# One VectorE maximum over two PSUM banks in place of one per bank, second context attention of a Perceiver kernel

## The reference

```python
q = (query @ Wq).reshape(b, sq, NUM_HEADS, HEAD_DIM).transpose(0, 2, 1, 3)   # 256 rows, 32 heads of 32
k = (key @ Wk).reshape(b, sk, NUM_KV_HEADS, HEAD_DIM).transpose(0, 2, 1, 3)  # 4096 context rows, 8 heads of 32
v = (value @ Wv).reshape(b, sk, NUM_KV_HEADS, HEAD_DIM).transpose(0, 2, 1, 3)
scores = jnp.einsum('bhqd,bhkd->bhqk', q, k) * scale                         # each key head serves 4 query heads
probs = jax.nn.softmax(scores, axis=-1)
out = jnp.einsum('bhqk,bhkd->bhqd', probs, v)
```

## Time and profile before

| | |
|---|---|
| time, median of 3 runs | 2255.72 us (2251.92 to 2257.29) |
| profiled execution: its time | 2258.47 us |
| profiled execution: its span | 2257.0 us |
| granted TensorE clock, mean over the span | 0.957 |
| VectorE maxima L1794 | 512 instructions, first at 1324.0 us, last at 1923.5 us |

### The profile page before, as it was taken

The page is one execution under the profiler, slowest core; times in us unless marked ns, Lnnn a source line. Parts: engine busy times, 40 slices in busy tenths (PEclk is TensorE's granted clock), DMA queues, the critical chain, the costliest instruction groups (busy, mean ns, idle before and its releaser), DMA issues.

```text
span 2257.0 us, 27306 instructions
## 1 busy us (share of the span) xinstructions
PE 2052.8 (91%) x10908; PEld 1502.6 (67%) x10908; DVE 1370.9 (61%) x2070; ACT 843.4 (37%) x1169; POOL 244.4 (11%) x131
## 2 busy tenths in 40 slices
PE   7899999999979999999989767999999999978978
PEld 5799999999968787877778644433333333356843
DVE  3454454454447878797666466666676667266455
ACT  2111111111126666656535212444434443735421
POOL 0000000000006555544000010000000000010000
PEclk9999999999989999999999878999999999989889
DMA  5443343342257656655443161011101110026042
GB/s 178 157 123 117 100 123 117 100 123 79 82 155 212 198 189 200 216 187 178 122 156 120 47 223 38 1 28 29 28 1 28 29 22 7 19 80 245 12 159 86
DMA packets 127869, 243.43 MB, mean 108 GB/s; under 512 B 16525, under 2 KB 79361, under 8 KB 120449
## 3 DMA queue, kind: packets, MB, share of 16 engines
q1 hardware_dynamic: 127745, 241.71, 34.5%
HBM read 177.70 MB, written 63.86 MB: 107 GB/s over the span
## 4 chain that ended last, share of the span: by engine, by line
PE 80%; DVE 11%; DMA 4%; ACT 3%; issue 2%; SPq 0%; POOL 0%; DVEq 0%; ACTq 0%
PE psum L1668 10%; PE psum L467 10%; PE psum L1636 7%; PE psum L1654 4%; PE psum L448 4%; PE psum L450 4%; PE psum L449 3%; PE psum L435 3%; PE psum L277 3%; PE psum L279 3%; PE psum L278 3%; DVE top L1794 3%; PE psum L812 3%; PE psum L814 2%; PE psum L813 2%; PE psum L827 2%
## 5 line engine op out<-in xcount | busy, mean ns | idle before, releaser
L1794 DVE TENSOR_REDUCE top<-psum 128x1 f32<-128x512 f32 x512 | 338.9, 688 | 142.6 <-PE psum L1636 140.8
L1735 ACT ACTIVATE probs_f<-psum 128x1024 f32<-128x1024 f32 x256 | 255.1, 1023 | 308.4 <-PE psum L1654 308.0
L600 DVE TENSOR_REDUCE top<-psum 128x2 f32<-128x512 f32 x272 | 186.5, 691 | 198.1 <-PE psum L435 197.9
L1636 PE MATMUL psum<-k_rows,q_rows 96*128 96x512 f32 x512 | 233.6, 484 | 50.1 <-DMA k_rows<-k_low 22.2
L1668 PE MATMUL psum<-probs_f,v_all 128*64 128x512 f32 x1024 | 274.0, 629 | 0.0
L1636 PEld LDWEIGHTS psum<-k_rows,q_rows 96*128 96x128 f32 x512 | 94.9, 197 | 232.1 <-DVE top L1794 179.3
L903 DVE TENSOR_TENSOR probs_low<-probs,probs_high 128x1024 fp32r<-128x1024 f32 x136 | 194.1, 1432 | 76.8 <-ACT probs L866 76.6
L865 ACT ACTIVATE probs_high<-psum 128x1024 fp32r<-128x1024 f32 x136 | 139.9, 1028 | 161.2 <-PE psum L814 148.3
L448 PE MATMUL psum<-c_high,w_high 128*128 128x256 f32 (+1 forms) x672 | 190.7, 284 | 3.2 <-issue 3.2
L449 PE MATMUL psum<-c_low,w_high 128*128 128x256 f32 (+1 forms) x672 | 190.6, 284 | 0.0
L450 PE MATMUL psum<-c_high,w_low 128*128 128x256 f32 (+1 forms) x672 | 190.5, 284 | 0.0
(11 more groups left out here) (356 smaller groups left out, 3701.3 us busy)
## 6 DMA issues: line engine op xcount, KB each, us to landing
wf_rows<-in_ffn_w_dram SPq DMA_DIRECT2D x42, 512.0 KB, 4.2
staged<-in_ctxT_dram SPq DMA_DIRECT2D x32, 512.0 KB, 5.1
wf_rows<-in_ffn_w_dram SPq DMA_DIRECT2D x8, 1376.0 KB, 7.6
q_dram<-wf_turned SPq DMA_DIRECT2D x42, 256.0 KB, 2.3
gate_up<-q_dram SPq DMA_DIRECT2D x10, 1024.0 KB, 8.1
value_high<-v_high SPq DMA_DIRECT2D x32, 256.0 KB, 3.7
value_low<-v_low SPq DMA_DIRECT2D x32, 256.0 KB, 4.6
k_rows<-k_high SPq DMA_DIRECT2D x16, 512.0 KB, 6.9
```

What stands on the lines that cost most here:

```text
L600: dve.tensor_reduce(top0[:, r0:r0 + 2, n], psum[:, bank, :].rearrange("p (i n) -> p i n", i=2), AX_X, ALU.max).then_inc(*b.bank_read.up())
L1636: pe.matmul(psum[:, bank, :], q_rows[0:3 * HD1, kv, rows * P:(rows + 1) * P], k_rows[kv % 2][0:3 * HD1, chunk * BANK:(chunk + 1) * BANK], ...
L1735: act.activation(probs[n % 4][:], psum[:, 2 * (n % 2):2 * (n % 2) + 2, :].rearrange("p b n -> p (b n)"), ACT.Exp, scale=scale).then_inc(*f ...
L1794: dve.tensor_reduce(top1[:, rows, chunk:chunk + 1], psum[:, 6 + m % 2, :], AX_X, ALU.max).then_inc(*f.max_read.up())
```

## The change

The even job of each two no longer waits for a single bank and no longer signals. It waits until VectorE has read both banks of the pair of jobs before; the odd job follows without a wait and signals for both. VectorE does nothing at even jobs and at odd ones reduces both banks in one instruction of 128 x (2 x 512) into two columns of `top1`. Counts of the semaphores are halved. The order of the calls on PE and the number of matmuls stay as they are.

```diff
@@ tensor_program, maximum @@
-                    if made >= 2:
-                        pe.wait_ge(*f.max_read.at(made - 1))
-                    pe.matmul(psum[:, bank, :], q_rows[0:3 * HD1, kv, rows * P:(rows + 1) * P],
-                              k_rows[kv % 2][0:3 * HD1, chunk * BANK:(chunk + 1) * BANK], start=True,
-                              stop=True).then_inc(*f.max_made.up())
+                    if m % 2 == 0 and made >= 2:
+                        pe.wait_ge(*f.max_read.at(made // 2))
+                    done = pe.matmul(psum[:, bank, :], q_rows[0:3 * HD1, kv, rows * P:(rows + 1) * P],
+                                     k_rows[kv % 2][0:3 * HD1, chunk * BANK:(chunk + 1) * BANK], start=True, stop=True)
+                    if m % 2:
+                        done.then_inc(*f.max_made.up())
                     made += 1
@@ vector_program, maximum @@
                     rows, chunk = divmod(m, NC1)
+                    if m % 2 == 0:
+                        return
                     read += 1
                     dve.wait_ge(*f.max_made.at(read))
-                    dve.tensor_reduce(top1[:, rows, chunk:chunk + 1], psum[:, 6 + m % 2, :], AX_X,
+                    dve.tensor_reduce(top1[:, rows, chunk - 1:chunk + 1], psum[:, 6:8, :], AX_X,
                                       ALU.max).then_inc(*f.max_read.up())
```

## The result

| | before | after |
|---|---|---|
| time, median | 2256.51 us (2251.92 to 2258.04, 4 runs) | 2595.59 us (2591.27 to 2621.42, 4 runs) |
| ratio, 95% interval | | 1.153 [1.1453, 1.1608] |
| span of the profiled execution | 2257.0 us | 2597.0 us |
| granted TensorE clock | 0.957 | 0.876 |

The account below looks back on a forecast made before the run. TensorE was taken as the bound: 2258.47 us plus 187 in the second pass's pairs and 42 in the first key head gave 2487.5, less 2.75 because the profiled execution was above the median, so 2485; range 2446 to 2560.

Parts of the forecast that it names:

- What bounds the kernel: Whole kernel: TensorE, busy 91% of the span, is where time counts; VectorE, busy 61%, is not saturated.
- the saving on VectorE is worth nothing: Reading instruction: VectorE gets 42 us shorter, but since it isn't the bound, this alone gains nothing.
- The read, 1.21 us: VectorE's maximum over 1024 elements, taken from a like reduction from SBUF at 1.206 us; 1.376 kept for the range.
- The hand-over, 1.71 us: Odd job's start to next even job's: 0.44 to the read, 1.21 read, 0.06 to the next weight load.
- The pairs at the full clock: Second pass, pairs of six: beginning even 7.08 us in place of 5.10; beginning odd 8.32, +3.22; seven key heads +187 us.
- The first key head: Its projection columns lengthen from 7.27 to 13.2 us at the low clock: +42 us in all.
- its split into hand-overs and low clock: First key head: +24 us at the full clock, +42 at the low clock that the prediction took.
- In the pairs ... I keep 1.00 there, as in the row that held: Second pass: granted clock stays 1.00 (2.4 GHz), as in an earlier stretch with PE busy 2.35 of 4 us.
- a sign of being wrong: Pairs of the second pass: the prediction is wrong if their clock row shows less than 0.9.
- a rival with 0.08: Clock falls to 1.2 GHz in the pairs too: about 3 us a pair, +231, 2716 us; partly, in between; chance 0.08.
- the terms named for its lower end, 12 and 18: Range of the whole kernel: 12 us from hand-over terms of 0.05 on 248, 18 down for the columns' clock.
- the 2.35 that I had leant on in the earlier trace: Kernel before: a stretch with PE busy 2.35 of 4 us kept clock 1.00; one with 2.02 fell to 0.51.

Follow-up runs that it names:

- zeros: Changed kernel plus 707 matmuls adding exactly zero to a bank, put on TensorE ahead of the even jobs' waits in the pairs: 2487.35 us, ratio to before 1.1037.

## Why the prediction was wrong, by its steps

- **What bounds the kernel, and that the saving on VectorE is worth nothing**: right. The wait alone, with the old reads, is already 8% slower.
- **The read, 1.21 us**: 1.225 measured. On 248 hand-overs that is 4 us.
- **The hand-over, 1.71 us**: 1.72.
- **The pairs at the full clock**: even 7.10 for 7.08; odd 8.54 for 8.32. Behind a wait, a weigh call follows its job after 0.43, where the walk took 0.33 from a row without a wait. With the clock held by zeros the second pass cost +189.0 for +187, and that close agreement is luck in part, as the table below shows: the odd pairs cost 6 us more than walked, the even ones 6 us less. In the kernel before not every even pair takes the 5.10 of the earlier trace rows; from the second key head on, the second and third take up to 5.7.
- **The first key head**: +44.0 for +42, and its split into hand-overs and low clock (24 and 18) came out as 17.7 by stage for the 18 (14.5 between the medians). Here the step that took the low clock from the earlier trace rows was right.
- **"In the pairs ... I keep 1.00 there, as in the row that held"**: this is the step that failed. The clock of the second pass was 0.76, below the 0.9 that the prediction had named as a sign of being wrong. Zeros in the waits took 108 us off, which is about what the forecast missed by (110.6). The prediction had this case as a rival with 0.08, "partly, in between" 2485 and 2716, and left most of it out of the range. The price it gave, about 3 us a pair, was also low for the odd pairs: 12.03 - 8.54 = 3.5.
- **The range**: the terms named for its lower end, 12 and 18, give 2455 and not 2446. That changed nothing.

Where in the second pass the time went, against the kernel before (us; a pair runs from its first job to the next pair's; the second pair of five runs on to the next key head's first score call; seven key heads, one profiled execution each):

| | walked | changed kernel | with 707 zeros |
|---|---|---|---|
| 35 pairs of six that begin even | +69.3 | +71.2 | +62.8 |
| 28 pairs of six that begin odd | +90.2 | +185.7 | +96.6 |
| first pair of five | +17.4 | +22.1 | +18.8 |
| second pair of five and what follows it | +10.4 | +19.6 | +10.3 |
| from a key head's first score call to its first job | 0 | +0.5 | +0.5 |

So the low clock was paid for mainly in the pairs that begin odd: 89 of the 110 us that the zeros gave back. The even ones kept 1.00 for the most part, as the prediction said of all. One key head of the changed kernel, four even pairs and then four odd, and under it the four odd pairs of the same key head with zeros:

```profile
1697.00:1725.00 28.00, 20.39 (x72) 8.18 (x72) 15.98 (x17) 8.19 (x8) 0.00 (x0) 1.00 0.00 1
1733.00:1780.00 47.00, 38.02 (x72) 13.45 (x71) 14.70 (x12) 8.19 (x8) 0.00 (x0) 0.50 0.00 0
```

```profile
1697.00:1731.00 34.00, 33.39 (x125) 14.97 (x124) 14.69 (x12) 8.18 (x8) 0.00 (x0) 1.00 0.00 0
```

What was wrong with the argument from the earlier trace rows is seen in three short stretches of the changed kernel's trace, all in even pairs:

```profile
1582.00:1586.00 4.00, 2.69 (x10) 1.46 (x12) 2.27 (x4) 1.58 (x2) 0.00 (x0) 1.00 0.00 0
...
1589.00:1593.00 4.00, 2.68 (x10) 1.55 (x12) 1.45 (x2) 1.48 (x2) 0.00 (x0) 1.00 0.00 0
1593.00:1597.00 4.00, 4.00 (x11) 0.89 (x7) 2.23 (x2) 0.57 (x1) 0.00 (x0) 0.57 0.00 0
```

Two stretches of four microseconds look alike, 2.69 and 2.68 us busy, more than the 2.35 that I had leant on in the earlier trace rows; behind the one the clock (1.00, so 2.4 GHz) stayed, behind the other it went to 1.2 GHz. One row in which the clock held, with other matmuls in it (projections beside the jobs, not scores and weighings), was taken for a rule. What makes the difference, between these two stretches and between even and odd pairs, stays open; only that more work in the waits holds the clock is shown. Once low, it stayed low for up to 55 us (1733.0 to 1787.6), while the waits went on. The Trainium skill, TensorE: Matmul & The Clock Gate, section A second HAM failure mode: psum-queue depth-cycling, says that short idleness between groups that cycle through banks makes the clock swing and costs throughput. This trace agrees, with a clock that went up and down all through the second pass, 0.76 in the mean, and some 110 us lost, and the rival deserved far more than 0.08.

## What to carry to other kernels

One wide instruction over both banks of a double buffer turns it into a single buffer: it saved VectorE 25 us that nobody waited for and put a hand-over of 1.72 us in TensorE's order, where only what stands between the last write and the next one covers it. Whoever has to couple two banks puts the two writes in one place and the longest other work behind them; that was worth 220 us here, clock included. And the repeated waits of a microsecond were paid for twice here: by themselves, and by the clock, which took another 110 us; before trusting that it holds, look for a stretch of the same kind of work, and give the fall a real chance in the range.

## What the runs showed of the hardware

- 707 useless matmuls, placed in waits, made the kernel 108 us faster, by holding the granted clock at 0.97 in place of 0.76; 280 of them already brought 97 us.
- The clock went with the order of the same work: 0.50 in four odd pairs of a key head whose four even pairs had kept 1.00, and 0.95 over the second pass when the two jobs of a bank pair stood in one place.
- A maximum over two banks (128 x 2 x 512) costs 1.225 us, close to the 1.206 of 1024 elements from SBUF, so no cost of crossing the bank shows. Two over one bank each, directly behind each other, take 1.29: a saved instruction is worth 0.06 or 0.07 us, and not the 0.15 that twice the mean of 0.688 suggests.
- From the start of the odd job to that of the even job that waits for its read, a hand-over took 1.72 us at the full clock.
